# A fourth wide group of x in place of a spread one, and the wide groups' partitions dealt out anew

## The chip, the cores and the metric

The kernel runs on one core of one Trainium2 chip. The metric is the device time of one execution in microseconds, as the median of repeated executions. The engines are named as in the profile: PE is TensorE (PEld its weight loads), DVE is VectorE, ACT is ScalarE, POOL is GpSimd, SP is SyncE, which here only issues transfers.

## The reference, cut to what matters

A recommendation tower over a batch of 512 with 39 embedding fields of 16 elements. Each sample's rows are looked up and stacked, and two layers of products of features follow:

```python
e = stack([tbl_f[ids[:, f]] for f in range(39)], axis=1)        # 512 x 39 x 16
z0 = einsum('bid,bjd->bdij', e, e).reshape(B, D, 39 * 39)
next_h, direct0 = split(relu(z0 @ W0), 2)                        # 64 and 64 of 128
z1 = einsum('bid,bjd->bdij', e, next_h).reshape(B, D, 39 * 64)
cur1 = relu(z1 @ W1)                                             # 128
z = concatenate([direct0, cur1]).sum over d                      # 512 x 192
h = relu(concat([z, dense_ctx]) @ W_top1 + b_top1)
y = relu(h @ W_top2 + b_top2) @ W_top3
```

The change is about z1: the product of each of the 39 fields of x with each of the 64 rows of next_h, and the matmul of those 2496 rows with W1.

## The kernel before, in words

The batch is cut into 16 chunks (CHUNKS) of 32 samples. A chunk's columns are its 32 samples times 16 elements, N = 512. All engines run one program each, in a fixed order, and semaphores join them.

**Gather.** For each chunk POOL issues 11 indirect DMAs (L266), 176 in all, which bring 117 rows each (39 fields for three samples) from the table into `found`, of which there are three buffers (BUFS). When a chunk's 11 have landed, ACT rounds them to a high part (`split`, L276) and DVE subtracts to get the low part (`split`, L384). SP then writes high, low and full values to a scratch tensor `x_rows` in HBM (`lay_out`, L201), waits for that, and reads the high and low rows back as `x_parts` (`place`, L210). Both sit in `bring(c)`.

**First layer.** PE forms sums of pairs of fields from `x_parts` (`add_up`, L470), ACT squares them (L285), and PE contracts the squares with W0 (`contract0`, L487). ACT evicts the result as `h`, twice, into partitions 0 to 63 and 64 to 127 (L292, L293), and as `direct` (L296), which DVE reduces (L414).

**Second layer.** A chunk has five groups (G = 5), counted through as n = 5c + g. A group multiplies up to eight fields with `h`: its operand is 128 partitions by four tiles of 512 columns, and each tile holds one field in 64 partitions and another in the other 64. So each group needs x with every field's row repeated over 64 partitions. This comes in one of two ways:

- *spread* (groups 0 and 3, `SPREAD`): PE does it, four matmuls with 32 rows each from `x_parts` into the PSUM tensor `spread` (`spread_out`, L500), which has one buffer, two groups of the order ahead;
- *wide* (groups 1, 2 and 4, `WIDE`): DMA does it, from HBM. SP reads four neighbouring rows of `x_rows` (8 KB together) into each of 64 partitions of `x_wide`, once for each half (`widen`, L219). Each wide group has one slot of `x_wide`, which SP fills for chunk c + 1 as soon as DVE has multiplied it for chunk c.

DVE multiplies x and `h` to `z` (`multiply`, L401). Groups other than `WHOLE` = 2 are split for exactness: ACT rounds to `z_hi` (`high_part`, L309), DVE subtracts to `z_lo` (`low_part`, L409), and PE contracts with three products for each tile (L511, L512, L519). Group 2 goes to PE unsplit (`contract1_whole`, L526 and L530), and its first tile uses 64 partitions only. ACT evicts the sum (`evict1`, L302) and DVE reduces it (L420).

**Order on DVE** in a chunk: multiply(1), low(0), multiply(2), low(1), reduce1 of the chunk before, multiply(3), multiply(4), low(3), multiply(0) of the next chunk, low(4), reduce0, split(c + 3), then multiply(1) again. ACT's split(c + 3) stands after high_part(4) and a square. DVE's and ACT's `split` wait in line: everything behind them on their engine waits too.

**Order on SP** after the start: for each chunk the `widen` calls of chunk c + 1, one for each wide group and each behind the multiply that frees its slot, then `bring(c + 3)`.

At the end the top network runs in a first part for 480 samples and a last part for 32.

Of the kernel before, what the change touches and what calls it, by code (L numbers as in the profile page):

```python
# [15 lines left out]
P = 128  # L16
# [3 lines left out]
HALF = 64  # L20
CB = 32
N = CB * D
# [12 lines left out]
QUADS = 4  # L35
# [7 lines left out]

G = 5
T1 = G * QUADS
SPREAD = [0, 3]
WIDE = [1, 2, 4]
SPREAD_FROM = [0, 4, 32, 12]
WIDE_FROM = [[8, 16], [28, 35], [20, 24]]


WHOLE = 2
# [4 lines left out]
BUFS = 3  # L57
# [11 lines left out]
def slot1(g):  # L69

    return QUADS * (VG if g == WHOLE else g - (g > WHOLE))
# [13 lines left out]
def build(nc, ids, base, table, select, w0a, w0b, mix, w1, wt1, bt1, wt2, bt2, wt3, dense, out):  # L85
    with ExitStack() as ctx:
# [14 lines left out]
        x_rows = nc.dram_tensor("x_rows", (BUFS, 3, FR, N), F32, kind="Internal")  # L101
# [91 lines left out]
        @block.sync  # L193
        def _(sp):
            def lay_out(c):

                b = c % BUFS
                sp.wait_ge(found_lo_done, c + 1)
                for s, w in enumerate(SET_COLS):
                    start = x_rows[b, 0, 0, GW * s:GW * s + 1]  # L200
                    sp.dma_start(bass.AP(start.tensor, start.offset, [[N, F], [FR * N, 3], [1, w]]),  # L201
                                 found[F * s:F * s + F, b, :, 0:w]).then_inc(rows_out[b], 16)

            def place(c):

                b = c % BUFS
                sp.wait_ge(rows_out[b], 16 * SETS * uses(c))
                for half in range(2):
                    start = x_rows[b, half, 0, 0:1]
                    sp.dma_start(x_parts[half:P:2, b, :].bitcast(F32),  # L210
                                 bass.AP(start.tensor, start.offset, [[N, 2 * STEP], [STEP * N, QUADS], [1, N]])
                                 ).then_inc(placed[b], 16)

            def widen(c, i):

                if c:
                    sp.wait_ge(multiplied, G * (c - 1) + WIDE[i] + 1)
                for a, f in enumerate(WIDE_FROM[i]):
                    sp.dma_start(x_wide[HALF * a:HALF * a + HALF, i, :],  # L219
                                 x_rows[c % BUFS, 2, f:f + QUADS, :].rearrange("f n -> (f n)").unsqueeze(0)  # L220
                                 .to_broadcast([HALF, QUADS * N])).then_inc(wide_in[i], 16)

            def bring(c):

                if c >= BUFS:
                    sp.wait_ge(placed[c % BUFS], 32 * uses(c - BUFS))
                    sp.wait_ge(multiplied, G * (c - BUFS + 1))
                lay_out(c)
                if c >= BUFS:
                    sp.wait_ge(spread_done, len(SPREAD) * (c - BUFS + 1))  # L230
                    sp.wait_ge(summed, ND * (c - BUFS + 1))
                place(c)

            sp.dma_start(ids_sb[:, :], ids).then_inc(ids_in, 16)
            sp.dma_start(w1_sb[:, :, :], w1).then_inc(w1_in, 16)
            for dst, src in ((wt1a_sb[:, :], wt1[HALF:HALF + P, :]),
                             (wt1b_sb[0:HALF, :], wt1[0:HALF, :]),
                             (wt1b_sb[HALF:, :], wt1[HALF + P:, :]),
                             (wt2_sb[:, :, :], wt2), (wt3_sb[:, :], wt3), (bt1_sb[:, :], bt1),
                             (bt2_sb[:, :], bt2), (feat_b[HALF:, :], dense)):  # L240
                sp.dma_start(dst, src).then_inc(mlp_in, 16)
            sp.wait_ge(filler_in, 16)
            bring(0)
            widen(0, 0)
            widen(0, 1)
            bring(1)
            widen(0, 2)
            bring(2)
            for c in range(CHUNKS - 1):
                for i in range(len(WIDE)):  # L250
                    widen(c + 1, i)
                if c + BUFS < CHUNKS:
                    bring(c + BUFS)
            sp.wait_ge(y_ready, 1)
            sp.dma_start(out, y_sb[:, :]).then_inc(out_done, 16)
            sp.wait_ge(out_done, 16)
# [123 lines left out]
        def _(dve):  # L380
# [6 lines left out]
            def multiply(n):  # L387
                c, g = n // G, n % G
                if g == 0:
                    dve.wait_ge(h_ready, 2 * (c + 1))  # L390
                if g in SPREAD:
                    dve.wait_ge(spread_done, len(SPREAD) * c + SPREAD.index(g) + 1)
                    x = spread[:, :, :]
                else:
                    dve.wait_ge(wide_in[WIDE.index(g)], 32 * (c + 1))
                    x = x_wide[:, WIDE.index(g), :].rearrange("p (t n) -> p t n", n=N)
                if n >= RING and is_v(n - RING):
                    dve.wait_ge(lo_done, v_count(n - RING))
                elif n >= RING:
                    dve.wait_ge(contracted1, n - RING + 1)  # L400
                nc.vector.tensor_tensor(z[:, n % RING], x,  # L401
                                        h[:, c % 2, :].unsqueeze(1).to_broadcast([P, QUADS, N]),
                                        ALU.mult).then_inc(multiplied, 1)
# [37 lines left out]
            for c in range(CHUNKS):  # L441
                for g in range(G):
                    n = G * c + g
# [185 lines left out]
def layout(inputs):  # L629
    ids = np.ascontiguousarray(inputs["ids"]).astype(np.int32)  # L630
    tables = [np.ascontiguousarray(inputs[f"tbl_{f}"]) for f in range(F)]

    by_set = np.zeros((SETS, F, CHUNKS, SLOTS), np.int32)
    for s, cols in enumerate(SET_COLS):
        w = cols // D
        rows = ids.reshape(CHUNKS, CB, F)[:, s * SLOTS:s * SLOTS + w]
        by_set[s, :, :, 0:w] = rows.transpose(2, 0, 1)
    starts = np.cumsum([0] + [t.shape[0] for t in tables])[:F].astype(np.float32)


    from_w0 = np.asarray(inputs["L0_rec_W0"]).reshape(F, F, P)
    w0a, w0b = np.zeros((2, T0 * P, P), np.float32)
    select = np.zeros((P, T0 + len(SPREAD), P), np.float32)
    mix = np.zeros((T0 * P, F), np.float32)
    for t, tile_pairs in enumerate(pairs()):
        for r, (i, j) in enumerate(tile_pairs, HALF if t == T0 - 1 else 0):
            w0a[t * P + r] = from_w0[i, j]
            if i != j:
                w0b[t * P + r] = from_w0[j, i]
            for f in (i, j):  # L650
                row = rows_of(f)[0]
                select[row:row + 2, t, r] = 1.0
                mix[t * P + r, f] = -1.0 if i != j else 2.0


    w1 = np.zeros((P, T1, P), np.float32)
    from_w1 = np.asarray(inputs["L0_rec_W1"]).reshape(F, HALF, P)
    for i, g in enumerate(SPREAD):
        for q in range(QUADS):
            for a in range(2):  # L660
                f = SPREAD_FROM[q] + 2 * i + a
                row = [r for r in rows_of(f) if r // 32 == q][0]
                select[row:row + 2, T0 + i, HALF * a:HALF * a + HALF] = 1.0
                w1[HALF * a:HALF * a + HALF, slot1(g) + q] = from_w1[f]
    spread_fields = {SPREAD_FROM[q] + k for q in range(QUADS) for k in range(2 * len(SPREAD))}
    for i, g in enumerate(WIDE):
        for a in range(2):
            for k in range(QUADS):
                f = WIDE_FROM[i][a] + k
                if f not in spread_fields:  # L670
                    w1[HALF * a:HALF * a + HALF, slot1(g) + k] = from_w1[f]

    def by_tile(a):
        return np.ascontiguousarray(a.reshape(T0, P, -1).transpose(1, 0, 2))

    return {
        "ids": by_set.reshape(GP, CHUNKS * SLOTS),
        "base": np.tile(starts, SETS).reshape(GP, 1),
        "table": np.concatenate(tables),
        "select": select.reshape(P, (T0 + len(SPREAD)) * P),  # L680
        "w0a": by_tile(w0a),
        "w0b": by_tile(w0b).reshape(P, T0 * P),
        "mix": by_tile(mix),
        "w1": w1,
        "wt1": np.asarray(inputs["W_top1"]),
        "bt1": np.ascontiguousarray(np.asarray(inputs["b_top1"]).reshape(M1 // P, P).T),
        "wt2": np.ascontiguousarray(np.asarray(inputs["W_top2"]).reshape(M1 // P, P, M2).transpose(1, 0, 2)),
        "bt2": np.ascontiguousarray(np.asarray(inputs["b_top2"]).reshape(M2 // P, P).T),
        "wt3": np.ascontiguousarray(np.asarray(inputs["W_top3"]).reshape(M2 // P, P).T),
        "dense": np.ascontiguousarray(np.asarray(inputs["dense_ctx"]).T),  # L690
    }
# [15 lines left out]
```

## Time and profile before

| | |
|---|---|
| median of 3 runs | 440.73 us (440.49 to 440.74) |
| profiled execution | 441.91 us, of which the span of the instructions is 439.9 us |
| PE busy | 407.8 us, 93% |
| DVE busy | 347.9 us, 79% |
| POOL busy | 285.5 us, 65% |
| ACT busy | 225.7 us, 51% |
| DMA engines, queue of SP | 61.7% of 16 engines' span, 60.75 MB |
| chain that ended last | PE 76%, POOL 12%, waits without a releaser 5%, DVE 3%, DMA 3% |

The busy shares are means over the whole span. The kernel has a start of about 90 us, in which gathers and the first transfers set the pace, then thirteen nearly equal chunks of 22.9 us, and an end of some 50 us without gathers. POOL's last gather ends at 342.5 us. A row of the trace gives a start in us from the beginning of the span, then a length.

### The profile page before, as it was taken

The page shows a single profiled execution, that of the slowest core. Times are in us where ns is not written, and L with a number is a line of the kernel's source. Part 1 is how long each engine was busy: PE and PEld are TensorE (multiplying, and loading weights), DVE is VectorE, ACT ScalarE, POOL GpSimd, SP SyncE. Part 2 cuts the span into 40 slices and gives each one's busy share as a digit, 9 for nine tenths or more (in the row PEclk, how much of TensorE's full clock was granted, in tenths as well). Part 3 has the DMA queues.
Part 4 walks back from the last instruction along what each step waited for, and adds up shares of the span by engine and source line. Part 5 has one row for each costly group of instructions (what it writes and reads, how often), then busy time and mean ns, then how long its engine had stood idle before and what let it go on. Part 6 is the DMA issues. An engine that isn't in the chain of part 4 may idle for free.

```text
span 439.9 us, 4140 instructions
## 1 busy us (share of the span) xinstructions
PE 407.8 (93%) x1490; PEld 250.4 (57%) x1490; DVE 347.9 (79%) x196; ACT 225.7 (51%) x224; POOL 285.5 (65%) x180
## 2 busy tenths in 40 slices
PE   0578699899999999999999999999999999996997
PEld 0444356446566656565756565666656565664564
DVE  0203755799999998989898989898989898999700
ACT  3114345365565647483747474747383747462422
POOL 5787878888888888888888888888888100000000
PEclk9989799999999999999999999999999999999899
DMA  8373629696959495959595977777786858570000
GB/s 282 97 180 76 133 62 217 155 208 153 213 116 213 111 208 112 212 110 216 108 220 120 200 142 171 157 178 153 176 165 157 180 138 197 127 161 0 1 0 2
DMA packets 23988, 64.03 MB, mean 146 GB/s; under 512 B 6755, under 2 KB 14904, under 8 KB 17695
## 3 DMA queue, kind: packets, MB, share of 16 engines
q1 hardware_dynamic: 17620, 60.75, 61.7%
q0 software_dynamic: 5632, 1.35, 3.1%
q10 hardware_dynamic: 715, 1.66, 1.1%
q8 instruction: 12, 0.20, 0.2%
q14 instruction: 9, 0.07, 0.1%
HBM read 59.88 MB, written 3.85 MB: 145 GB/s over the span
## 4 chain that ended last, share of the span: by engine, by line
PE 76%; POOL 12%; issue 5%; DVE 3%; DMA 3%; ACT 0%; DVEq 0%
PE acc L487 15%; POOL found L266 12%; PE acc L519 12%; PE acc L512 11%; PE acc L511 11%; PE acc L530 9%; PE sums L470 6%; PE acc L526 4%; PE spread L500 3%; DVE z_lo L409 3%; DMA found<-in_table_dram,rows_sb 2%; PE spread L559 2%; PE sums L550 1%; DVE z L401 1%; DMA base_sb<-in_base_dram 1%
## 5 line engine op out<-in xcount | busy, mean ns | idle before, releaser
L266 POOL DMA_INDIRECT found<-in_table_dram,rows_sb x176 | 285.3, 1621 | 56.7 <-issue 53.3
L309 ACT ACTIVATE z_hi<-z 128x2048 fp32r<-128x2048 f32 x64 | 122.4, 1912 | 83.1 <-DVE z L401 78.4
L409 DVE TENSOR_TENSOR z_lo<-z,z_hi 128x2048 fp32r<-128x2048 f32 x64 | 146.2, 2286 | 14.6 <-ACT z_hi L309 8.8
L487 PE MATMUL acc<-squares,w 128*128 128x512 f32 (+1 forms) x224 | 111.2, 614 | 0.0
L511 PE MATMUL acc<-z_hi,w_hi 128*128 128x512 f32 x256 | 106.2, 415 | 4.5 <-issue 2.3
L401 DVE TENSOR_TENSOR z<-x_wide,h 128x2048 f32<-128x2048 f32 x48 | 109.6, 2283 | 0.0
L512 PE MATMUL acc<-z_hi,w_lo 128*128 128x512 f32 x256 | 100.2, 391 | 0.0
L401 DVE TENSOR_TENSOR z<-spread,h 128x2048 f32<-128x2048 f32 x32 | 73.2, 2286 | 20.8 <-issue 17.0
L285 ACT ACTIVATE squares<-sums 128x1024 f32<-128x1024 f32 x64 | 58.4, 913 | 59.7 <-PE sums L470 45.7
L519 PE MATMUL acc<-z_lo,w_hi 128*128 128x512 f32 x256 | 83.3, 447 | 1.8 <-DVE z_lo L409 1.8
L519 PEld LDWEIGHTS acc<-z_lo,w_hi 128*128 128x128 f32 x256 | 48.5, 191 | 26.2 <-issue 15.1
L511 PEld LDWEIGHTS acc<-z_hi,w_hi 128*128 128x128 f32 x256 | 48.1, 188 | 19.7 <-issue 6.3
L487 PEld LDWEIGHTS acc<-squares,w 128*128 128x128 f32 (+1 forms) x224 | 42.4, 195 | 29.2 <-issue 25.4
L512 PEld LDWEIGHTS acc<-z_hi,w_lo 128*128 128x128 f32 x256 | 48.1, 188 | 13.3 <-issue 3.3
L470 PE MATMUL sums<-x_parts,select_sb 128*128 128x512 f32 x112 | 42.8, 453 | 5.8 <-DMA x_parts<-x_rows 3.9
L530 PE MATMUL acc<-z,w_sb 128*128 128x512 f32 x96 | 45.5, 610 | 0.0
L530 PEld LDWEIGHTS acc<-z,w_sb 128*128 128x128 f32 x96 | 16.9, 189 | 27.4 <-issue 27.4
L470 PEld LDWEIGHTS sums<-x_parts,select_sb 128*128 128x128 f32 x112 | 20.3, 195 | 18.6 <-issue 9.9
L302 ACT ACTIVATE cur<-acc 128x512 f32<-128x512 f32 x16 | 9.6, 597 | 26.4 <-PE acc L519 26.4
L420 DVE TENSOR_REDUCE feat_a<-cur 128x32 f32<-128x512 f32 x16 | 10.9, 680 | 13.9 <-ACT cur L302 13.9
L526 PE MATMUL acc<-z,w_sb 64*128 64x512 f32 x32 | 18.1, 647 | 0.0
L384 DVE TENSOR_TENSOR found<-found 117x176 fp32r<-117x176 f32 x16 | 5.5, 342 | 15.4 <-issue 9.5
(44 smaller groups left out, 144.5 us busy)
## 6 DMA issues: line engine op xcount, KB each, us to landing
x_wide<-x_rows SPq DMA_DIRECT2D x96, 512.0 KB
x_parts<-x_rows SPq DMA_DIRECT2D x32, 128.0 KB
found<-in_table_dram,rows_sb POOLq DMA_INDIRECT x176
x_rows<-found SPq DMA_DIRECT2D x32, 80.4 KB
w_sb<-in_w_dram SPq DMA_DIRECT2D x1, 1280.0 KB, 6.8
x_rows<-found SPq DMA_DIRECT2D x16, 73.1 KB
z<-in_select_dram ACTq DMA_DIRECT2D x1, 576.0 KB, 7.5
wt_sb<-in_wt_dram SPq DMA_DIRECT2D x1, 512.0 KB
```

Of the source, the lines that this page charges most:

```text
L266: pool.indirect_dma_start(out=found[:, b, 2, s * D:s * D + D], out_offset=None, in_=table, in_offset=bass.IndirectOffsetOnAxis(ap=rows_sb[ ...
L285: nc.scalar.activation(squares[rows, q % RING0, 0:n, :], sums[rows, 0:n, :], ACT.Square).then_inc(squared, 1)
L309: nc.scalar.activation(z_hi[:, n % RING], z[:, n % RING], ACT.Copy).then_inc(hi_done, 1)
L401: nc.vector.tensor_tensor(z[:, n % RING], x, h[:, c % 2, :].unsqueeze(1).to_broadcast([P, QUADS, N]), ALU.mult).then_inc(multiplied, 1)
L409: nc.vector.tensor_tensor(z_lo[:, n % RING], z[:, n % RING], z_hi[:, n % RING], ALU.subtract).then_inc(lo_done, 1)
L470: last = nc.tensor.matmul(sums[:, a, :], select_sb[:, t, :], x_parts[:, c % BUFS, :], start=True, stop=True)
L487: last = nc.tensor.matmul(acc0[:, :], w0[rows, t, :], squares[rows, q % RING0, a, :], start=(t == 0), stop=(t == T0 - 1))
L511: nc.tensor.matmul(acc1[:, :], w1_hi[:, t, :], z_hi[:, r, a, :], start=(t == 0), stop=False)
L512: last = nc.tensor.matmul(acc1[:, :], w1_lo[:, t, :], z_hi[:, r, a, :], start=False, stop=False)
L519: last = nc.tensor.matmul(acc1[:, :], w1_hi[:, slot1(g) + a, :], z_lo[:, r, a, :], start=False, stop=(g == G - 1 and a == QUADS - 1))
L526: nc.tensor.matmul(acc1[:, :], w1_sb[0:HALF, VT, :], z[0:HALF, r, 0, :], start=False, stop=False)
L530: last = nc.tensor.matmul(acc1[:, :], w1_sb[:, VT + a, :], z[:, r, a, :], start=False, stop=False)
```

## The change

Group 3, until now a spread one, becomes wide. The fields are dealt out again over the groups. In a wide group the four fields that stood in partitions 0 to 63 now stand in the middle 64 (32 to 95), and the other four stand in the lower and the upper 32. A wide group is so filled by three transfers (64, 32 and 32 partitions) instead of two of 64, and by four for group 2, whose first tile has one field only. `wide_in` counts follow. At the start SP also fills the new group's slot, before `bring(2)`. `spread_out` is unchanged, and is called for group 0 alone, because it goes by `SPREAD`.

```diff
-SPREAD = [0, 3]
-WIDE = [1, 2, 4]
-SPREAD_FROM = [0, 4, 32, 12]
-WIDE_FROM = [[8, 16], [28, 35], [20, 24]]
+SPREAD = [0]
+WIDE = [1, 2, 3, 4]
+SPREAD_FROM = [0, 14, 16, 37]
+WIDE_FROM = [[2, 6], [30, 33], [10, 18], [22, 26]]
...
                 if c:
                     sp.wait_ge(multiplied, G * (c - 1) + WIDE[i] + 1)
-                for a, f in enumerate(WIDE_FROM[i]):
-                    sp.dma_start(x_wide[HALF * a:HALF * a + HALF, i, :],
-                                 x_rows[c % BUFS, 2, f:f + QUADS, :].rearrange("f n -> (f n)").unsqueeze(0)
-                                 .to_broadcast([HALF, QUADS * N])).then_inc(wide_in[i], 16)
+
+                def spread_row(parts, t, f, count):
+                    sp.dma_start(x_wide[parts, i, t * N:(t + count) * N],
+                                 x_rows[c % BUFS, 2, f:f + count, :].rearrange("f n -> (f n)").unsqueeze(0)
+                                 .to_broadcast([parts.stop - parts.start, count * N])).then_inc(wide_in[i], 16)
+
+                middle, outer = WIDE_FROM[i]
+                spread_row(slice(32, 96), 0, middle, QUADS)
+                if WIDE[i] == WHOLE:
+                    spread_row(slice(0, 32), 0, middle, 1)
+                    spread_row(slice(0, 32), 1, outer + 1, QUADS - 1)
+                else:
+                    spread_row(slice(0, 32), 0, outer, QUADS)
+                spread_row(slice(96, P), 0, outer, QUADS)
...
             widen(0, 2)
+            widen(0, 3)
             bring(2)
...
-                    dve.wait_ge(wide_in[WIDE.index(g)], 32 * (c + 1))
+                    dve.wait_ge(wide_in[WIDE.index(g)], 16 * (4 if g == WHOLE else 3) * (c + 1))
```

The host's layout of `select` and `w1` follows the new places of the fields.

## Rows read from the trace of the kernel before

**Rows 1.** Busy time by engine, count, clock, DMA share, GB/s: one steady chunk.

```profile
205.72:228.60 22.88, 22.88 (x87) 14.19 (x86) 21.52 (x13) 13.37 (x14) 19.53 (x12) 1.00 0.77 164
```

**Rows 2.** The same view for the gathers of L266 alone.

```profile
0.00:205.30 205.30, 168.18 (x110) 0.98 0.72 161
205.30:228.20 22.90, 19.52 (x11) 1.00 0.78 165
```

**Rows 3.** The chain that ended last, in a steady chunk: start, length, link.

```profile
335.71 0.43 PE spread L500 x2
```

**Rows 4.** Timeline of DVE and PE, second half of a chunk: start, length, instruction.

```profile
222.30 2.28 DVE L409 TENSOR_TENSOR z_lo<-z,z_hi 128x2048 fp32r<-128x2048 f32 x1
224.50 0.68 DVE L420 TENSOR_REDUCE feat_a<-cur 128x32 f32<-128x512 f32 x1
225.10 2.28 DVE L401 TENSOR_TENSOR z<-spread,h 128x2048 f32<-128x2048 f32 x1
...
226.48 1.07 PE L519 MATMUL acc<-z_lo,w_hi 128*128 128x512 f32 x4
```

**Rows 5.** Timeline, first half of a chunk, all engines but PE.

```profile
204.19 1.00 POOL L266 DMA_INDIRECT found<-in_table_dram,rows_sb  x1 [0.30 <-issue]
...
207.70 0.59 ACT L296 ACTIVATE direct<-acc 64x512 f32<-64x512 f32 x1
...
209.04 2.29 DVE L401 TENSOR_TENSOR z<-spread,h 128x2048 f32<-128x2048 f32 x1
...
210.08 1.00 POOL L266 DMA_INDIRECT found<-in_table_dram,rows_sb  x1 [0.30 <-issue]
210.55 1.90 ACT L309 ACTIVATE z_hi<-z 128x2048 fp32r<-128x2048 f32 x1
...
212.49 2.29 DVE L409 TENSOR_TENSOR z_lo<-z,z_hi 128x2048 fp32r<-128x2048 f32 x1 [1.15 <-issue]
212.69 2.96 POOL L266 DMA_INDIRECT found<-in_table_dram,rows_sb  x1 [0.30 <-issue]
...
214.70 0.67 DVE L414 TENSOR_REDUCE feat_b<-direct 64x32 f32<-64x512 f32 x1
215.06 0.34 ACT L276 ACTIVATE found<-found 117x176 fp32r<-117x176 f32 x1
215.44 0.34 DVE L384 TENSOR_TENSOR found<-found 117x176 fp32r<-117x176 f32 x1
215.70 2.29 DVE L401 TENSOR_TENSOR z<-x_wide,h 128x2048 f32<-128x2048 f32 x1
```

**Rows 6.** Timeline of POOL beside the rows of groups 4 and 5.

```profile
215.96 2.90 POOL L266 DMA_INDIRECT found<-in_table_dram,rows_sb  x1 [0.30 <-issue]
...
225.76 0.99 POOL L266 DMA_INDIRECT found<-in_table_dram,rows_sb  x1 [0.30 <-issue]
227.06 1.00 POOL L266 DMA_INDIRECT found<-in_table_dram,rows_sb  x1 [0.30 <-issue]
```

**Rows 7.** Last gathers of chunks 0 and 3 (POOL), and ACT's splits of them.

```profile
17.73 1.00 POOL L266 DMA_INDIRECT found<-in_table_dram,rows_sb  x1 [0.30 <-issue]
...
20.16 0.35 ACT L276 ACTIVATE found<-found 117x176 fp32r<-117x176 f32 x1 [8.31 <-DMA found<-in_table_dram,rows_sb]
...
70.47 1.00 POOL L266 DMA_INDIRECT found<-in_table_dram,rows_sb  x1 [0.30 <-issue]
...
79.45 0.35 ACT L276 ACTIVATE found<-found 117x176 fp32r<-117x176 f32 x1 [4.85 <-DMA found<-in_table_dram,rows_sb]
```

**Rows 8.** SP's issues after a split: the layout, then the wide transfers.

```profile
215.86 1.18 SPq L201 DMA_DIRECT2D x_rows<-found  x3
...
219.83 3.67 SPq L219 DMA_DIRECT2D x_wide<-x_rows  x4
```

**Rows 9.** Busy time by engine, clock, DMA share, GB/s in stretches with wide transfers.

```profile
66.00:79.00 13.00, 12.89 (x47) 7.83 (x45) 5.86 (x4) 6.53 (x6) 10.55 (x9) 1.00 1.03 220
221.00:222.00 1.00, 1.00 (x7) 0.49 (x6) 1.00 (x1) 0.00 (x0) 0.70 (x2) 1.00 1.01 344
```

More of the change, by code:

```diff
@@ L664, in layout @@
                 w1[HALF * a:HALF * a + HALF, slot1(g) + q] = from_w1[f]
-    spread_fields = {SPREAD_FROM[q] + k for q in range(QUADS) for k in range(2 * len(SPREAD))}
     for i, g in enumerate(WIDE):
[L667 to L671, printed above, removed]
+        middle, outer = WIDE_FROM[i]
+        for k in range(QUADS):
+            first = g == WHOLE and k == 0
+            for p in range(HALF if first else P):
+                f = (middle if first or 32 <= p < 96 else outer) + k
+                w1[p, slot1(g) + k] = from_w1[f, p % HALF]
     def by_tile(a):
```

## Prediction

> **What bounds the kernel now.** I began with the page's shares (PE 93%, DVE 79%, POOL 65%), which are means, and went on to the stretches of the steady part. In one chunk of 22.88 us PE is busy for all of it, DVE for 21.52, POOL for 19.53 [rows 1]. So PE sets the pace, at the full granted clock (1.00, the 2.4 GHz level). The chain of waits agrees: it runs through PE's matmuls with no gap, and `spread_out` is a link in it. DVE is close behind. Its operations start 2.20 us apart when nothing holds them; nine of them, reduce0 (0.74 to the next start), split (0.26) and reduce1 (0.60) make 19.80 + 1.60 = 21.40 us [rows 4, 5]. The rest of 22.88 is two pauses around multiply(0) and low(4), where DVE waits for ACT and PE.
>
> POOL looks idle by 3.3 us a chunk, and is not. All its idle time is the 0.30 us between two gathers: 11 x 0.30 + 19.53 = 22.83, a whole chunk. It never waits for a buffer. What to see is the length of a gather. One that starts while DVE multiplies from `spread` takes 0.99 or 1.00 us (210.08, 225.76). One that starts under a DVE operation with both inputs in SBUF lasts until 0.87 us after that operation's end: 212.69 + 2.96 = 215.65, the low part ends at 214.78; 215.96 + 2.90 = 218.86, the multiply from `x_wide` ends at 217.99 [rows 5, 6]. I compared all gathers after 50 us with DVE's operations, and this fits every one. So each DVE operation of that kind lets one gather through. A chunk has seven (four low parts, three wide multiplies) and gives 7 gathers; the two spread multiplies with the pauses beside them give two each. That is exactly the 11 that a chunk needs, and exactly 11 are issued per chunk [rows 2]. The lead of the gathers neither grows nor shrinks: the 110th, last of chunk 9, ends at 205.19, and its split is at 215.06, 9.9 us later [rows 2, 5].
>
> The Trainium skill (SBUF — State Buffer, "Who interferes with whom") says that a DVE instruction with two SBUF inputs contends with a GpSimd instruction that reads SBUF, and one with at most one such input does not. By that rule a multiply from PSUM leaves POOL alone and one from `x_wide` does not; the trace agrees (0.99 us against 1.9 to 2.96 us).
>
> **The change part by part.**
>
> *PE loses four matmuls a chunk.* On the chain they are 0.43 us [rows 3], 0.44 in most chunks: PE's chunk becomes 22.88 - 0.44 = 22.44 us. DVE needs 21.40 and is not in the way. The multiply itself costs the same from PSUM and from SBUF, 2.28 us [rows 4, 5].
>
> *DMA carries 1 MB more a chunk.* Four groups of 1 MB (1.05 million bytes) instead of three. With wide transfers alone in the queue the rate is 220 GB/s [rows 9], 4.8 us a group; 4 x 4.8 = 19.2 us. In the stretch where transfers to all partitions mix with wide ones it is 344 GB/s [rows 9], 3.0 us a group. The new transfer to the middle 64 partitions touches both halves of the partitions, the two of 32 do not. I take half at 344 and half at 220: 1.5 + 2.4 = 3.9 us a group, 15.6 a chunk. Bounds 12 and 19.2; with some 1.5 us for rows out and in both are below 22.44. The slot for group g is filled about a whole chunk before its use, so no multiply waits. SP issues 13 transfers instead of 6, at 0.59 to 0.92 us each (3.67 us for four, a wait included) [rows 8]; 8 us of 22, hidden in SP's waits for DVE.
>
> The Trainium skill (SBUF — State Buffer, "Door 1: The DMA port swizzle") says that partitions 0 to 63 reach 8 of the 16 DMA ports, about 218 GB/s, and its port table puts 32 to 95 on all 16. The measured 220 agrees with the first; by the page's 436 GB/s for 16 ports a group would take 1.2 + 2.4 = 3.6 us, an estimate, instead of 3.9.
>
> *POOL loses a slot a chunk.* Under multiply(3) two gathers start now, at 225.76 and 227.06 [rows 6]. With x in SBUF the first is held until multiply(3) ends, 227.38 + 0.87, and the next falls under multiply(4) as before. Eight operations give 8, the stretch at multiply(0) two: 10 gathers where 11 are needed. This is the term that decides. While the lead lasts it costs nothing. Each chunk the last gather of a chunk moves one slot (1.3 to 2.2 us) later and its split comes 0.44 earlier. In slots: split(4) has 8.6 us left, split(5) 4.8, split(6) 3.9, split(7) 2.6; at split(8) the last gather is the one held under low(4).
>
> Then DVE and ACT stand at `split` until it lands, and wait in line there for every chunk up to 15. Landing to ACT's split took 20.16 - 18.73 = 1.43 us with idle queues, and 79.45 - 71.47 = 8.0 behind 3 MB of wide transfers [rows 7]. The wide transfers of the chunk end before this gather is issued, so I take 1.43. From the end of low(4), at X: gather ends X + 0.87, ACT splits at X + 2.30, DVE 0.38 later, multiply(1) 0.26 after that: X + 2.94. Now it is X + 0.92 (215.70 against 214.78) [rows 5]. Stall 2.02 us. With PE no longer ahead, ACT still holds low(4) by 0.16: `direct` at 207.70 + 0.60, square 0.92, z_hi 1.91, so 211.18 against 209.04 - 0.22 + 2.20 = 211.02 [rows 5]. The chunk becomes 21.40 + 0.16 + 2.02 = 23.58 us. Does POOL keep it? 8 held gathers, one at multiply(0) (the stretch is shorter now), two in the stall: 11. It is a steady state, 0.70 us a chunk slower than before.
>
> *Start.* Multiply(3) of chunk 0 takes a slot too; chunk 3's last gather, the chain's link there (70.47, split at 79.45) [rows 7], starts some 1.3 us later, less 0.4 from PE's shorter order: +0.9. Bounds: 0, and +4.5 if it lands with the end of 4 MB at 4.8 (64.1 + 19.2 = 83.3 against 79).
>
> **The sum**, from split(3) on: start +0.9; to split(7) four chunks at -0.44, -1.8; the eighth stall, of which PE's distance from low(1) absorbs 226.48 - 224.58 - 0.44 = 1.4 [rows 4], chunk of 22.44 + 0.6 against 22.88, +0.15; seven chunks to split(15), 7 x 0.70 = +4.9; the last two without gathers, -0.9. Together +3.3. The profiled execution of 441.91 would be 445.2; the median is 1.2 below it, so 440.73 + 3.3 = 444.0.
>
> With landings of 3 to 8 us the stall falls in other slots. The same count gives chunks of 23.5 to 24.2 on the mean, and +4 to +8.
>
> **The rivals.**
>
> *POOL does not bind (faster).* The stall itself can open a slot: if split comes only 0.4 to 0.55 us late, a gather slips in between low(4) and multiply(1) (now the start at 215.96 misses by 0.26 us) [rows 6], both starts at multiply(0) stay, and DVE's spare 22.44 - 21.40 = 1.04 takes the stall. It decides at a landing of about 2.7 us. Or a gather under back-to-back operations finds room that I don't see. Then +0.9 - 13 x 0.44 = -4.8: 435.9 us. Against it: the lock has held in every chunk to 0.01 us, and a slot costs 2.2.
>
> *DMA binds.* The new transfers run at 220 GB/s after all, and gathers land when the burst ends, as at 79.45. Then a chunk is 19.2 + 4.4 from split to the next burst (219.83 - 215.44) [rows 5, 8], 23.6, plus 0.8 for landing and split: 24.4, or 1.5 x 12 = +18. If only part of the gathers wait, half of that: 450 to 459.
>
> *The effects cancel.* Stalls are shorter or come later (a larger lead, or chunks alternating between 10 and 12 slots near 22.9): 440 to 441.6. In that case the change does little: PE's 0.44 us is handed to `split`.
>
> **How the numbers follow.** POOL binds and queues are calm or moderate, 442 to 448.5: 0.52, with 444.0 the likeliest. POOL does not bind: 0.22. Cancel: 0.10. DMA binds: 0.12. Something else, 0.04. Range 435.5 to 450 holds the first three; the likeliest case's own range is 442 to 448.5. A measurement tells 0.2%, 0.9 us: faster 0.23, same 0.09, slower 0.68.
>
> **What would show it.** L500 falls from 128 to 64 matmuls. Multiply(3) reads `x_wide`, at 2.28 us. Gathers beside it take about 1.9 to 2.9, none 0.99. Until about 190 us chunks are 22.44 long and PE has no idle time; gathers per chunk 10. After that ACT's L276 and DVE's L384 show idle time, released by the gather's DMA, about 2 us a chunk, PE about 1 us idle a chunk, POOL 11 gathers in 23.4 to 24 us and its last gather past 350. DMA share of a chunk about 0.8, with bins over 300 GB/s. The prediction is wrong if gathers keep coming 11 in 22.44 us, or if the split never waits; it is wrong the other way if `x_wide` rows stand under DVE's waits or the bins stay at 220 GB/s.

## The result, and the profile after

The change makes the kernel slower: 450.06 us against 440.61 us for the kernel before beside it, ratio 1.0198 (95% interval 1.0153 to 1.0242; the quotient of the two medians is 1.021). A second comparison gave 448.80 us, ratio 1.0194 (1.0122 to 1.0266). The kernel before scatters in the later sets, from 438.9 to 453.1 us over 37 executions, so the table below also gives each kernel's median over those executions alone that lie within 1.5% of its fastest. The prediction said 444.0, slower, by a gather of POOL that no longer fits into a chunk. Direction and mechanism held. The size did not: +9.4 us on the median, 8.0 between the two profiled executions (449.99 and 441.91), where 3.3 was forecast. The median lies above the 442 to 448.5 of the likeliest case, and 0.06 us above the end of the whole range, 435.5 to 450.

The page of the changed kernel: the busy times, the chain that ended last, and the groups that stand for the change.

```profile
PE 402.3 (90%) x1426; PEld 248.1 (55%) x1426; DVE 346.7 (77%) x196; ACT 226.8 (51%) x224; POOL 297.5 (66%) x180
...
q1 hardware_dynamic: 21972, 77.54, 67.1%
...
POOL 66%; issue 16%; PE 7%; DVE 7%; DMA 3%; ACT 1%; POOLq 0%; DVEq 0%; ACTq 0%
...
L395 DVE TENSOR_TENSOR found<-found 117x176 fp32r<-117x176 f32 x16 | 5.5, 345 | 40.5 <-ACT found L287 40.3
...
L287 ACT ACTIVATE found<-found 117x176 fp32r<-117x176 f32 x16 | 5.6, 348 | 39.7 <-DMA found<-in_table_dram,rows_sb 39.7
```

The chain has moved from PE to POOL: 66%, and most of the 16% "issue" are the 0.30 us between its gathers. ACT stands 39.7 us at `split` for gathers to land (13.2 before, all at the start; now 21.0 at the start and 18.7 from chunk 5 on), and DVE 40.3 behind it. SP's queue moves 77.5 MB instead of 60.8, 28% more, in 67.1% of the DMA engines' span instead of 61.7%: the new deal of the partitions is quicker (deal_only, below, has the old 60.8 MB in the new deal, in 49.4%). POOL's share of busy time, 66%, is hardly higher than before. That is the trap of this profile: after its first gather POOL is never idle for more than 0.31 us in either kernel, and what changed is how long a gather is held.

POOL and ACT in the changed kernel; here 230.26 to 232.54 is multiply(3), now from `x_wide`, 239.22 to 241.51 is low(4), and 235.92 is the start of the last gather of chunk 10.

```profile
230.92 2.49 POOL L277 DMA_INDIRECT found<-in_table_dram,rows_sb  x1 [0.30 <-issue]
233.72 1.90 POOL L277 DMA_INDIRECT found<-in_table_dram,rows_sb  x1 [0.30 <-issue]
235.92 1.90 POOL L277 DMA_INDIRECT found<-in_table_dram,rows_sb  x1 [0.30 <-issue]
238.12 1.00 POOL L277 DMA_INDIRECT found<-in_table_dram,rows_sb  x1 [0.30 <-issue]
239.42 2.96 POOL L277 DMA_INDIRECT found<-in_table_dram,rows_sb  x1 [0.30 <-issue]
```

```profile
126.50 0.35 ACT L287 ACTIVATE found<-found 117x176 fp32r<-117x176 f32 x1 [0.45 <-DMA found<-in_table_dram,rows_sb]
...
220.22 0.35 ACT L287 ACTIVATE found<-found 117x176 fp32r<-117x176 f32 x1 [2.50 <-DMA found<-in_table_dram,rows_sb]
...
246.20 0.35 ACT L287 ACTIVATE found<-found 117x176 fp32r<-117x176 f32 x1 [4.29 <-DMA found<-in_table_dram,rows_sb]
```

The gather at 230.92 is held until 233.41. It answers to the two free ones of [rows 6]. The last one ends at 237.82, ACT's split of that chunk comes at 246.20, 8.4 us later. Busy time by engine, count, clock, DMA share and GB/s from one split to the next, for five chunks and for all twelve from chunk 3's split to chunk 15's:

```profile
104.10:126.50 22.40, 22.40 (x83) 14.18 (x83) 21.73 (x13) 13.49 (x14) 19.35 (x11) 1.00 0.83 230
126.50:148.86 22.36, 22.36 (x83) 14.17 (x82) 21.43 (x12) 13.50 (x13) 19.23 (x11) 1.00 0.84 221
220.22:246.20 25.98, 24.26 (x85) 14.30 (x83) 21.43 (x12) 13.49 (x14) 22.32 (x13) 1.00 0.79 186
246.20:267.82 21.62, 19.08 (x68) 11.52 (x69) 21.17 (x12) 13.38 (x13) 18.57 (x11) 1.00 0.83 203
...
82.52:362.15 279.63, 270.00 (x966) 168.00 (x967) 257.20 (x144) 161.63 (x157) 233.69 (x126) 0.99 0.83 207
```

The first two full chunks, with waits of 0.45 and 0.56 us at their ends, take 22.4 us, less than the 22.88 of [rows 1]. Chunks with a longer wait take up to 26, and the twelve 23.30 on the mean. Waits begin at split(5), and from there to split(15) the ten chunks take 235.65 us, 23.57 each. POOL is busy 233.7 us for its 126 gathers, 1.85 each; in the kernel before 224.6 for 127 in the same stretch of work, 1.77 each. Where the 8.0 us went, from the splits of the two traces:

| stretch | before | after | difference |
|---|---|---|---|
| start, to chunk 3's split | 79.45 | 82.52 | +3.1 |
| chunk 3's split to chunk 15's | 272.89 | 279.63 | +6.7 |
| chunk 15's split to the end of the span | 87.56 | 85.75 | -1.8 |

### The profile page after: what moved, and what is told of

Read it like the earlier page. It is cut to its first block, busy times and chain, and to the rows that moved or that the text cites. A ratio compares the mean times of both kernels' runs of the same rounds, so it can differ in the third digit from the quotient of the medians.

```text
span 447.9 us, 4124 instructions
## 1 busy us (share of the span) xinstructions
PE 402.3 (90%) x1426; PEld 248.1 (55%) x1426; DVE 346.7 (77%) x196; ACT 226.8 (51%) x224; POOL 297.5 (66%) x180
## 3 DMA queue, kind: packets, MB, share of 16 engines
q1 hardware_dynamic: 21972, 77.54, 67.1%
## 4 chain that ended last, share of the span: by engine, by line
POOL 66%; issue 16%; PE 7%; DVE 7%; DMA 3%; ACT 1%; POOLq 0%; DVEq 0%; ACTq 0%
POOL found L277 66%; DVE z_lo L420 4%; DVE z L412 2%; DMA found<-in_table_dram,rows_sb 2%; PE spread L570 2%; PE sums L559 1%; PE sums L561 1%; PE acc L530 1%; PE acc L541 1%; DMA base_sb<-in_base_dram 1%; POOLq L86 0%; PE spread L577 0%; PE acc L523 0%; PE acc L522 0%; ACT z_hi L320 0%
## 5 line engine op out<-in xcount | busy, mean ns | idle before, releaser
L277 POOL DMA_INDIRECT found<-in_table_dram,rows_sb x176 | 297.3, 1689 | 56.6 <-issue 53.3
L412 DVE TENSOR_TENSOR z<-x_wide,h 128x2048 f32<-128x2048 f32 x64 | 144.8, 2282 | 0.0
L530 PE MATMUL acc<-z_lo,w_hi 128*128 128x512 f32 x256 | 82.4, 443 | 9.1 <-DVE z_lo L420 9.1
L530 PEld LDWEIGHTS acc<-z_lo,w_hi 128*128 128x128 f32 x256 | 47.5, 189 | 36.8 <-DVE z_lo L420 15.9
L412 DVE TENSOR_TENSOR z<-spread,h 128x2048 f32<-128x2048 f32 x16 | 36.5, 2284 | 16.7 <-ACT h L304 16.7
L481 PE MATMUL sums<-x_parts,select_sb 128*128 128x512 f32 x112 | 40.8, 435 | 5.8 <-DMA x_parts<-x_rows 3.9
L395 DVE TENSOR_TENSOR found<-found 117x176 fp32r<-117x176 f32 x16 | 5.5, 345 | 40.5 <-ACT found L287 40.3
L287 ACT ACTIVATE found<-found 117x176 fp32r<-117x176 f32 x16 | 5.6, 348 | 39.7 <-DMA found<-in_table_dram,rows_sb 39.7
```

What stands on the lines that cost most here:

```text
L277: pool.indirect_dma_start(out=found[:, b, 2, s * D:s * D + D], out_offset=None, in_=table, in_offset=bass.IndirectOffsetOnAxis(ap=rows_sb[ ...
L412: nc.vector.tensor_tensor(z[:, n % RING], x, h[:, c % 2, :].unsqueeze(1).to_broadcast([P, QUADS, N]), ALU.mult).then_inc(multiplied, 1)
L481: last = nc.tensor.matmul(sums[:, a, :], select_sb[:, t, :], x_parts[:, c % BUFS, :], start=True, stop=True)
L530: last = nc.tensor.matmul(acc1[:, :], w1_hi[:, slot1(g) + a, :], z_lo[:, r, a, :], start=False, stop=(g == G - 1 and a == QUADS - 1))
```

## The experiments

Theory A is the prediction's: POOL has one gather slot a chunk fewer than it needs. Theory B, the rival to be told from it: the fourth MB makes gathers land late, and slots don't matter. All times are in us. The first two columns have all executions of the kernel, the next two the medians of those within 1.5% of the fastest, of the kernel and of the kernel before run beside it; the last is their quotient.

| kernel | median | lowest to highest | near the fastest | before, near the fastest | quotient |
|---|---|---|---|---|---|
| changed kernel | 450.06 | 448.44 to 450.63 | 450.06 | 440.61 | 1.021 |
| changed kernel again | 448.80 | 447.25 to 452.06 | 448.80 | 440.87 | 1.018 |
| idle_mb | 461.54 | 459.43 to 463.56 | 461.54 | 441.58 | 1.045 |
| slot_only | 446.63 | 444.90 to 448.62 | 446.63 | 441.58 | 1.011 |
| psum_operand | 434.40 | 432.67 to 436.68 | 434.40 | 441.58 | 0.984 |
| halves | 464.39 | 461.79 to 466.69 | 464.39 | 441.58 | 1.052 |
| h_in_psum | 435.67 | 433.58 to 437.64 | 435.67 | 441.08 | 0.988 |
| ten_gathers | 435.77 | 432.93 to 441.12 | 434.51 | 441.08 | 0.985 |
| deal_only | 449.29 | 440.63 to 452.28 | 443.92 | 441.08 | 1.006 |
| before once more | 444.41 | 439.22 to 452.82 | 440.37 | 441.08 | 0.998 |

psum_operand, h_in_psum, idle_mb and halves don't overlap with the kernel before at all: its 37 executions beside these runs lie between 438.9 and 453.1 us (more on that scatter below).

**The traffic alone, in the old deal.** A fourth pair of wide transfers is added to the kernel before, into a buffer that nobody reads:

```diff
+            def widen_idle(c):
+                if c:
+                    sp.wait_ge(multiplied, G * (c - 1) + 4)
+                    sp.wait_ge(idle_in, 32 * c)
+                for a in range(2):
+                    sp.dma_start(x_idle[HALF * a:HALF * a + HALF, :],
+                                 x_rows[c % BUFS, 2, 4 * a:4 * a + QUADS, :]...).then_inc(idle_in, 16)
...
                 for i in range(len(WIDE)):
+                    if i == 2:
+                        widen_idle(c + 1)
                     widen(c + 1, i)
```

> The kernel before, with a fourth pair of wide transfers (1 MB a chunk, two of 64 partitions) into a buffer that nobody reads: all traffic of the change, no operation changed. Theory A (gather slots: POOL loses one of 11 because the fourth wide multiply holds it): the 11 slots are all there, so no split waits in the steady part; 440.6 us, or up to 444 if only the start (chunk 3's gathers landing behind 4 MB) is later. Theory B (traffic: gathers land late behind the fourth MB): splits wait as in the changed kernel, 447 to 452 us.

Measured: 461.54 us. Neither theory said that. No split waits for a gather after chunk 3 (the gathers' lead, from the end of a chunk's last gather to its split, grows to 36 us by chunk 15), so this is not theory B; and it is not near 440 either. SP's own waits in this kernel (what waited, for whom, us in total, times, longest) and two of its chunks:

```profile
SPq L209 <- DMA x_rows<-found: 103.1, 8, 14.5
SPq L200 <- DVE found L399: 62.9, 13, 13.8
```

```profile
223.91:249.20 25.29, 22.94 (x86) 14.18 (x85) 21.68 (x13) 13.37 (x14) 21.32 (x14) 1.00 0.89 192
200.03:223.91 23.88, 23.47 (x89) 14.59 (x88) 21.22 (x12) 13.37 (x15) 20.22 (x13) 1.00 0.89 190
```

The rows out of `lay_out` stand in SP's queue behind 4 MB at some 220 GB/s, `place` waits for them up to 14.5 us, and PE waits for `x_parts`, 19.8 us in 13 waits. The transfers bind by themselves: 24.5 us a chunk on the mean (split 3 to split 15, 293.97 us by 12). That is a third mechanism, the prediction's rival "DMA binds", with rows out in place of gathers.

**The changed kernel in the old deal.** The fourth group stays, and every wide group is filled by two transfers into partitions 0 to 63 and 64 to 127:

```diff
-                spread_row(slice(32, 96), 0, middle, QUADS)
...
+                spread_row(slice(0, HALF), 0, first, QUADS)
+                spread_row(slice(HALF, P), 0, second, QUADS)
...
```

The count that `multiply` waits for and the host's layout of `w1` follow.

> The changed kernel with the wide groups filled as before, two transfers each into partitions 0 to 63 and 64 to 127. If the middle and outer deal carries 1 MB in 4.5 us instead of 4.8 to 5: bursts of 4 MB end 1 to 2 us later, gathers land later, each chunk 0.5 to 1.5 us longer; 455 to 465 us. If the deal does nothing: 450 us.

Measured: 464.39 us, and again SP waits at `place`: 74.0 us in 7 waits, up to 13.7. Splits 5 and 7 also wait for gathers, 3.7 and 3.2 us, so both limits show in this kernel. The deal is worth about 14 us to the changed kernel. It carries four groups in 16 us, where the old deal at 220 GB/s needs 19. In the changed kernel's burst the rate is 262 GB/s, 4.0 us a group:

```profile
202.00:218.00 16.00, 16.00 (x60) 9.78 (x59) 15.83 (x9) 9.60 (x9) 13.87 (x8) 1.00 1.03 262
```

**The slot alone.** The kernel before, with group 3 multiplied from the slot of group 4 and without its `spread_out`, so that group 3's fields of x are wrong. No transfer is added:

```diff
-                    dve.wait_ge(wide_in[WIDE.index(g)], 32 * (c + 1))
-                    x = x_wide[:, WIDE.index(g), :]...
+                    dve.wait_ge(wide_in[WIDE.index(4 if g == 3 else g)], 32 * (c + 1))
+                    x = x_wide[:, WIDE.index(4 if g == 3 else g), :]...
...
-                    if (n + 2) % G in SPREAD and n + 2 < G * CHUNKS:
+                    if (n + 2) % G == 0 and n + 2 < G * CHUNKS:
...
```

> The kernel before, with group 3 multiplied from the x_wide slot of group 4 and its spread_out left out (so its fields of x are wrong): the PE saving and the lost slot of the change, with no added transfer. Theory A (slots): POOL issues 10 gathers in a 22.44 us chunk, the lead runs out by chunk 8 or so, then splits wait; 444 to 449 us. Theory B (traffic): 3 MB as before, so no split waits and PE's 0.44 us a chunk is the whole effect, 434 to 436 us.

Measured: 446.63 us (444.9 to 448.6 in ten executions), theory A's range. With 64.0 MB as before, the chain is 67% POOL and the waits are there: all eleven splits from chunk 5 on wait, 20.4 us of the 35.2 below (who waited for whom, us in total, times, longest; two waits are at the start). One chunk takes 24.16 us, and the ten from split(5) to split(15) 23.66 on the mean, about as long as in the changed kernel:

```profile
DVE found L384 <- ACT found L276: 36.8, 13, 7.6
ACT found L276 <- DMA found<-in_table_dram,rows_sb: 35.2, 13, 8.3
```

```profile
218.20:242.36 24.16, 22.77 (x83) 13.94 (x82) 21.43 (x12) 13.49 (x14) 20.80 (x12) 1.00 0.74 156
```

Against the kernel before near its fastest slot_only is 5.1 us slower, the changed kernel 9.4. Of the difference between the two, 2.5 us stand at the start: split(3) comes at 80.03 here and at 82.52 there. The profiled execution of slot_only, 448.62 us, is its slowest of ten, so how much the fourth MB adds later on isn't shown.

**The slot given back, the traffic kept.** The changed kernel, with group 3's second operand read from PSUM (the values are wrong):

```diff
+                other = spread[:, 0, :] if g == 3 else h[:, c % 2, :]
                 nc.vector.tensor_tensor(z[:, n % RING], x,
-                                        h[:, c % 2, :].unsqueeze(1).to_broadcast([P, QUADS, N]),
+                                        other.unsqueeze(1).to_broadcast([P, QUADS, N]),
...
-                    pe.wait_ge(multiplied, G * (c - 1) + SPREAD[-1] + 1)
+                    pe.wait_ge(multiplied, G * (c - 1) + 4)
```

> The changed kernel, with the second operand of group 3's multiply read from PSUM (a tile of spread, so the values are wrong) instead of h in SBUF: same transfers, same PE work, but only one input in SBUF. Theory A (slots): gathers beside multiply(3) take 1.0 us again, 11 or more a chunk, no split waits in the steady part, 22.44 us a chunk; 436 to 440 us, the upper end if the start stays 3 us late. Theory B (traffic): nothing changes, 449 to 451 us.

Measured: 434.40 us. This decides between the theories, because nothing in it differs from the changed kernel but where one operand lies, and that PE's next `spread_out` waits for multiply(3), which now reads `spread`. Multiply(3) of one chunk, the gathers beside it, and a chunk from split to split:

```profile
201.64 2.28 DVE L413 TENSOR_TENSOR z<-x_wide,spread 128x2048 f32<-128x2048 f32 x1
```

```profile
202.29 1.00 POOL L277 DMA_INDIRECT found<-in_table_dram,rows_sb  x1 [0.30 <-issue]
203.60 1.00 POOL L277 DMA_INDIRECT found<-in_table_dram,rows_sb  x1 [0.30 <-issue]
```

```profile
191.60:213.86 22.26, 22.26 (x82) 14.07 (x81) 21.42 (x13) 13.37 (x14) 18.91 (x12) 1.00 0.87 217
```

The multiply costs the same, two gathers pass beside it, no split waits from chunk 4 on, and the lead stands at 10.6 us. The DMA share is 0.87, higher than in the changed kernel, and harms nothing.

**One gather fewer.** The changed kernel with 10 gathers a chunk from chunk 3 on; the rows of the last slot are left out:

```diff
-                for s in range(SLOTS):
+                for s in range(SLOTS if c < BUFS else SLOTS - 1):
...
```

> The changed kernel with 10 gathers a chunk instead of 11 from chunk 3 on (the last slot's rows are left out, so old rows are used for two samples of 32). Theory A (slots): 10 are needed and 10 slots are there in 22.3 us; no or nearly no split waits after the start; 434 to 438 us. Theory B (traffic): 10 or 11 small gathers behind 4 MB land equally late, 447 to 451 us.

Measured: 435.77 us, chunks of 22.26, no wait from chunk 4 on and a constant lead of 11.9 us: exactly ten slots for ten gathers. By itself it would not tell much, since it also takes a little traffic away; beside psum_operand it gives the same time by another way.

**The deal alone.** The kernel before, its three wide groups filled the new way (the constants of before, `spread_row` of after):

> The kernel before with its three wide groups filled the new way (middle 64, lower and upper 32), groups 0 and 3 spread as before. PE sets the pace with 22.88 us a chunk and no multiply waits for x_wide, so the deal alone gives nothing in a calm execution: 440 to 441 us. The bursts of 3 MB end earlier (about 13 us instead of 14.5 to 15), so gathers land with more to spare: chunk 3's split up to 1.5 us earlier, and fewer executions above 442.

Measured: a median of 449.29 us, from executions at 440.63, 447.21, 451.37 and 452.28. The profiled one is the 440.63, with chunks of 22.86 us, and no split waits after chunk 3. For a profile of one near 450 it ran twice more:

> The kernel before with the wide groups filled the new way, again, to see one of its executions near 450 us. If gather slots are the cause (theory A at its edge: 11 slots for 11 gathers), an execution near 450 shows splits that wait for gathers and about 10 gathers in a 22.9 us chunk, and one near 440 shows none. If something else is, splits don't wait in it either.

> The same kernel as deal_look_1, for a second execution. Theory A: near 450 us splits wait for gathers, near 440 us none does. Otherwise splits wait in neither.

Both came out near 440, 441.47 and 438.94 us, and no split waits in either after chunk 3. The kernel before, run again for the same reason, gave 439.2 to 452.8 in eight executions, and its profile fell on the fastest:

> The kernel before once more, for its profile: its times beside the last runs lay between 439.5 and 453.1 us. Theory A (slots): POOL has exactly 11 slots for 11 gathers and a constant lead, so an execution in which the gathers once land later than the lead keeps waiting at split; a slow execution would show splits that wait for gathers, a fast one none.

So in executions near 440 the deal gives nothing in time, as expected for a kernel that PE paces, although SP's queue then takes 49.4% to 51.7% of the DMA engines' span for its 60.8 MB, where it took 61.7%. What the executions near 450 are was not seen.

**The changed kernel again:**

> The changed kernel once more, beside the kernel before on this chip: 448 to 451 us. Theory A: splits wait for gathers in most chunks from 5 on, with 10 or 11 gathers a chunk.

Measured: 448.80 us; from chunk 5 on, ten of eleven splits wait for gathers.

**A version that beats both, by little.** In the changed kernel `spread` lies idle between multiply(0) and the next `spread_out`. ACT copies h there, and the wide multiplies read it from PSUM. Nothing is left out:

```diff
+                    if g == G - 1 and c + 1 < CHUNKS:
+                        nc.scalar.activation(spread[:, 0, :], h[:, (c + 1) % 2, :], ACT.Copy).then_inc(h_copied, 1)
...
+                if g == 1 and c:
+                    dve.wait_ge(h_copied, c)
+                other = spread[:, 0, :] if g and c else h[:, c % 2, :]
...
-                    pe.wait_ge(multiplied, G * (c - 1) + SPREAD[-1] + 1)
+                    pe.wait_ge(multiplied, G * c)
```

> The changed kernel; from chunk 1 on ACT copies h into the first tile of spread (idle in PSUM between multiply(0) and the next spread_out), and the four wide multiplies read it there, so they have one input in SBUF. Nothing is left out. Only the four low parts of a chunk hold a gather then. Theory A (slots): POOL needs about 4 x 2.2 + 7 x 1.3 = 17.9 us for 11 gathers, its lead grows, no split waits after chunk 3; chunks of 22.3 us (the copy's 0.6 us on ACT delays split by as much, DVE has 0.9 to spare); 433 to 436 us, faster than both kernels. Theory B (traffic): unchanged traffic, 449 to 451 us.

Measured: 435.67 us, 1.2% under the kernel before; its slowest execution, 437.64, lies below the fastest of the kernel before, 438.96. A chunk, the copy, and DVE's split behind it:

```profile
191.70:213.96 22.26, 22.26 (x83) 14.07 (x82) 21.49 (x12) 13.89 (x16) 18.91 (x12) 1.00 0.85 189
```

```profile
213.44 0.60 ACT L372 ACTIVATE spread<-h 128x512 f32<-128x512 f32 x1
...
214.34 0.37 DVE L398 TENSOR_TENSOR found<-found 117x176 fp32r<-117x176 f32 x1 [0.59 <-ACT found L288]
```

The copy delays `split` by some 0.6 us in every chunk, and DVE's spare time takes it: PE has no idle time. POOL's lead grows from 10.5 us at chunk 4 to 24.3 at chunk 15.

## Why the prediction was right, and where it was off

**The decisive term**, a slot lost a chunk, was right in place and mechanism: slot_only has it without the traffic and takes 446.6 us, psum_operand has the traffic without it and takes 434.4. The lead runs out at split(5), where the first wait after the start stands, 0.45 us, and not at split(8). So the sign "until about 190 us chunks are 22.44 long" failed.

**PE's saving** was put at 0.44 us a chunk and is 0.62: chunks without waits take 22.26. The chain of the kernel before and that of psum_operand at the same place show why. The single `add_up` matmul behind the spread ones took 0.44 on the chain, and takes 0.23 without them. (L470 and L482 are the same line.)

```profile
313.26 0.44 PE sums L470
```

```profile
220.12 0.23 PE sums L482
```

**The landing** is the term that was mis-sized. I took 1.43 us from a gather's end to ACT's split, with the queues idle, because the transfers would be done by then: "The wide transfers of the chunk end before this gather is issued". They are not. The burst that begins at 202 ends about 219, and split comes at 220.22; the gather had ended at 213.62.

```profile
217.00:218.00 1.00, 1.00 (x6) 0.79 (x5) 0.91 (x2) 0.72 (x1) 1.00 (x1) 1.00 0.94 198
218.00:219.00 1.00, 1.00 (x6) 0.84 (x5) 0.00 (x0) 0.00 (x0) 0.69 (x2) 1.00 0.61 131
219.00:220.00 1.00, 1.00 (x6) 0.81 (x5) 0.00 (x0) 0.00 (x0) 0.70 (x2) 1.00 0.14 39
```

Over the nine splits from chunk 5 on that show a wait, the distance was 6.4 to 8.4 us, about the 8.0 of [rows 7] that I had set aside as the busy case. It is not always the end of the burst that lets them land: at splits 7, 9, 10, 14 and 15 the burst had ended (DMA share 0.00 to 0.35 in the half microsecond before), at splits 3, 5, 6, 8 and 12 it was still running (0.95 to 1.33 in the half microsecond behind). Why a gather takes that long beside a burst is not shown. With this landing the lead runs out three chunks earlier, and waits are 0.3 to 4.3 us, in no steady pattern: a chunk of 26 us is followed by one of 21.6.

The steady state itself was forecast at 23.58 us a chunk and came out at 23.57, as a mean over ten chunks and not seven. That is partly luck: it was counted with the same wait of 2.02 in every chunk and a landing of 1.43. But the rate hardly depends on the landing: the same ten chunks take 23.60 in the changed kernel's second trace and 23.66 in slot_only, where the distance is 1.9 to 5.9 us. What the longer landing cost is three more chunks in this state, 3 x 0.70, and the saving of the chunks up to split(7), -1.8 + 0.15, of which only 0.1 came. Split 3 to 15 cost +6.7 us against 4 x (-0.44) + 0.15 + 7 x 0.70 = +3.3. The prediction's own line for landings of 3 to 8 us, chunks of 23.5 to 24.2 and +4 to +8, has the profiled difference of 8.0 at its edge and the median's 9.4 outside.

**The start** was put at +0.9 and is +3.1. The last gather of chunk 3 ends at 74.46 instead of 71.47 and its split comes 8.1 us later (8.0 before), so nearly all of it is POOL's. Two gathers before it are held, and I counted only the first:

```profile
60.46 2.73 POOL L277 DMA_INDIRECT found<-in_table_dram,rows_sb  x1 [0.30 <-issue]
...
70.49 2.67 POOL L277 DMA_INDIRECT found<-in_table_dram,rows_sb  x1 [0.31 <-issue]
```

```profile
70.00 2.29 DVE L420 TENSOR_TENSOR z_lo<-z,z_hi 128x2048 fp32r<-128x2048 f32 x1 [1.08 <-ACT z_hi L320]
```

The first stands under multiply(3). The second stands under low(4), which now starts at 70.00; before it started at 71.91, and the gather at 70.47 still passed free. The earlier order that I had booked as a gain of 0.4 us put a DVE operation in front of a gather, 1.7 us. psum_operand has the second hold and not the first, and its split comes at 81.28.

**The end**, from chunk 15's split, came out at -1.8 instead of -0.9; two chunks and part of a third at 0.62 account for most of it.

**The rivals.** "POOL does not bind" was false here, and its price was about right: psum_operand takes 434.4 where 435.9 was given. "DMA binds" was false for the changed kernel, by its deal alone: halves takes 464.4 and idle_mb 461.5, above even the 450 to 459 of that rival. My 3.9 us a group for the new deal was close to the 4.0 measured, though half at 344 and half at 220 GB/s was a guess: no run times the middle transfer by itself. By the port rule of the Trainium skill (SBUF — State Buffer, "Door 1: The DMA port swizzle") the estimate was 3.6. The measurement lies above it; the direction, that the mix with the middle 64 partitions goes faster than two halves, agrees (262 against 220 GB/s).

**Left open.** The kernel before and deal_only scatter from 439 to 453 us between executions, while psum_operand and h_in_psum stay within 432.7 to 437.6 us over ten. Both scattering kernels have eleven slots for eleven gathers, the others room to spare. That speaks for the slots, but ten_gathers, with none to spare, once took 441.1, the changed kernel and slot_only, a slot short, keep within 5 us, and no profile of an execution near 450 was had. It is not shown.

## What to carry to other kernels

An engine that is never idle in the trace, although its share is 65%, is a second bound at its edge: look at how long its single instructions take and beside what, and count slots in a chunk before work is moved. Here a change that takes 0.6 us a chunk from the engine that sets the pace cost 9.4 us in all by where an operand lies; one operand in PSUM instead of SBUF gave it back. And small transfers beside a burst land late, here 6.4 to 8.4 us after their issue ends and not 1.4, so a lead that looks long against an idle queue can be too short.

## What the runs showed of the hardware

A multiply on DVE with x in SBUF and the other operand in PSUM takes 2.28 us, as with both in SBUF, and holds no gather. A gather under a DVE operation with both inputs in SBUF ends 0.87 us after that operation, which the changed kernel shows again (233.41 against 232.54). Mostly one gather passes with each such operation, but not always: at 47.96 us of the kernel before one was held for 4.69 us, through multiply(2) and the low part behind it, and ended 0.88 us after the second.

The same 4 MB a chunk cost 24.5 us in transfers to partitions 0 to 63 and 64 to 127 (idle_mb), and fitted into 22.26 in transfers to 32 to 95, 0 to 31 and 96 to 127 (psum_operand). I had not expected the old deal to bind through the rows out, which wait in the same queue, before any wide operand was late by more than 2.1 us in idle_mb and 2.6 in halves.
